# A transformer block with attention and experts: the first norms of batches 1 to 3 share their statistics, and norms, square sums, reciprocals and projections are issued in smaller pieces

## The reference, cut to what matters

```python
x = x + attention(layernorm(x))          # layernorm over the 128 features, eps 1e-5
def attention(z):
    k, q, v = z @ Wk, z @ Wq, z @ Wv     # 16 heads of 8
    k = head_norm(k) * kln_w + kln_b     # over the 8 features of each head
    q = head_norm(q) * qln_w + qln_b
    dot = einsum(q, k) / sqrt(8), causal mask, softmax over keys
    return einsum(softmax, v) @ Wo + bo
```

## Time and profile before

| | us |
|---|---|
| median of 3 timed runs | 2811.04 (2809.29 to 2815.23) |
| the profiled execution's own time | 2812.77 |
| its span | 2811.0 |
| TensorE busy | 2606.5 (93%) |
| VectorE busy | 1777.8 (63%) |
| ScalarE busy | 1602.0 (57%) |
| GpSimd busy | 819.7 (29%) |

### The profile page before, as it was taken

One profiled execution on the slowest core, in us unless ns is written; L12 is line 12 of the kernel. 1 busy time (PEld: TensorE's weight loads), 2 busy tenths in 40 slices (PEclk: granted clock), 3 DMA queues, 4 the chain that ended last, 5 costly groups with the idle time before them and its releaser, 6 DMA issues. The chain is left out here.

```text
span 2811.0 us, 54937 instructions
## 1 busy us (share of the span) xinstructions
PE 2606.5 (93%) x18814; PEld 1697.9 (60%) x18814; DVE 1777.8 (63%) x4103; ACT 1602.0 (57%) x2918; POOL 819.7 (29%) x1181
## 2 busy tenths in 40 slices
PE   5899998988599889999999999999999999995997
PEld 3555565554488745565555556555555555554886
DVE  7777777784566655555655556555556655556666
ACT  2666666776544455555555556565566555554443
POOL 4152423426154311111111111122122123322642
PEclk7999999999899989999999999999999999998998
DMA  6500000001434268888888888877888788885222
GB/s 110 87 12 16 16 16 9 16 13 35 124 121 149 74 153 199 196 195 194 202 194 196 195 195 191 187 181 180 188 189 194 181 201 200 202 202 197 72 87 86
DMA packets 193508, 383.24 MB, mean 136 GB/s; under 512 B 46305, under 2 KB 101738, under 8 KB 191882
## 3 DMA queue, kind: packets, MB, share of 16 engines
q1 hardware_dynamic: 184650, 362.55, 54.1%
q0 software_dynamic: 8640, 17.84, 1.8%
HBM read 38.10 MB, written 39.86 MB: 28 GB/s over the span
## 5 line engine op out<-in xcount | busy, mean ns | idle before, releaser
L3060 DVE STREAM_TRANSPOSE m_turned<-m_sig 128x1024 f32<-128x1024 f32 x512 | 613.6, 1227 | 434.0 <-ACT m_sig L2816 198.7
L2653 PE MATMUL m_v_ps<-m_sig,m_tok 128*64 128x512 f32 x2048 | 468.3, 599 | 0.0
L2666 PE MATMUL m_v_ps<-m_sigT,m_tok 128*64 128x256 f32 x4064 | 461.7, 380 | 3.7 <-DMA m_sigT<-m_turned 3.4
L2637 PE MATMUL m_f_ps<-m_swap,m_own 64*128 64x512 f32 x1536 | 426.1, 404 | 16.4 <-DMA m_swap<-m_own 8.2
L885 ACT ACTIVATE a_prob<-a_bank 128x512 f32<-128x512 f32 (+1 forms) x640 | 328.5, 568 | 175.5 <-PE a_bank L703 172.6
L2637 PE MATMUL m_f_ps<-m_own,m_swap 64*128 64x512 f32 x1536 | 426.3, 404 | 0.0
L2666 PEld LDWEIGHTS m_v_ps<-m_sigT,m_tok 128*64 128x64 f32 x4064 | 289.2, 137 | 202.1 <-issue 52.6
L2926 POOL TENSOR_TENSOR m_own<-m_uv,m_own 128x1024 fp32r<-128x1024 f32 x64 | 152.0, 2374 | 816.4 <-ACT m_own L2792 816.4
L2830 ACT ACTIVATE m_sig<-m_f_ps 128x1024 f32<-128x1024 f32 x256 | 248.3, 1022 | 246.0 <-issue 148.2
L2637 PEld LDWEIGHTS m_f_ps<-m_swap,m_own 64*128 64x128 f32 x1536 | 271.6, 186 | 99.9 <-ACT m_sig L2816 25.9
L2653 PEld LDWEIGHTS m_v_ps<-m_sig,m_tok 128*64 128x64 f32 x2048 | 135.8, 137 | 265.4 <-issue 265.0
(11 more groups left out here) (507 smaller groups left out, 4318.4 us busy)
## 6 DMA issues: line engine op xcount, KB each, us to landing
m_sigT<-m_turned SPq DMA_DIRECT2D x2042, 128.0 KB, 2.3
m_swap<-m_own SPq DMA_DIRECT2D x64, 256.0 KB, 3.3
f_t_rows<-f_sent_rows SPq DMA_DIRECT2D x142, 65.0 KB, 2.0
f_sent_rows<-a_proj SPq DMA_DIRECT2D x34, 260.0 KB, 8.8
k_apart<-a_kT SPq DMA_DIRECT2D x128, 64.0 KB, 2.0
m_swap<-m_own SPq DMA_DIRECT2D x64, 128.0 KB, 3.2
f_h<-back_rows SPq DMA_DIRECT2D x8, 512.0 KB, 5.0
rows<-back_rows SPq DMA_DIRECT2D x6, 512.0 KB, 4.2
```

The source lines that it names most:

```text
L2637: mm = pe.matmul(f_ps[s][:, cols], tile_of(u[rows, :], j + s * SIDE), v[rows, cols], start=start, stop=stop)
L2653: mm = pe.matmul(v2_ps[h * RANK:(h + 1) * RANK, :], tok[p][:, 0, j + s * SIDE, :], sig[j % 2][s][:, h * HALF:(h + 1) * HALF], start=(j == ...
L2666: mm = pe.matmul(v1_ps[h * RANK:(h + 1) * RANK, g * 2 * P:(g + 1) * 2 * P], tok[p][:, 1, jj, :], sigT[g][:, :, 2 * h:2 * h + 2, jj, :].rea ...
L3060: dve.transpose(turned[g][:, :, q, :, :], sig[j % 2][s][:, :].rearrange("p (t j a) -> p j t a", j=4, a=STACK)).then_inc(turn_ready, 1)
```

## The change

- The statistics of the 24 tiles of batches 1 to 3 are taken in the first group, two tiles at each of the slots 8, 10, ..., 30; moments, root and reciprocal for all 24 follow once, at slots 33, 35 and 37 of the same group. They live in the buffers of the later norms (`x_mean`, `x_dev`, `x_rstd`, `stats`), which nothing else uses at that time.
- The norm of a batch is issued in four pieces of two tiles at slots 1, 3, 5 and 7 of g = 1; the turns are at slots 10 and 12; the projections one at a time at slots 14, 16, 18, 21, 23, 26, 29 and 31. Before the first of them ScalarE waits for the stacked queries of the batch before.
- In g = 2 the square sums of the keys are at slot 5 and those of the queries at slot 6, each with its own scaling; the reciprocal of the keys stays at slot 9, that of the queries is at slot 14. The opening does the same in halves.

```diff
+        STATS_AT = tuple(range(8, 32, 2))
+        PROJECT_AT = (14, 16, 18, 21, 23, 26, 29, 31)
...
+                if first and i in STATS_AT:
+                    yield "token_stats", STATS_AT.index(i)
+                if first and i in (33, 35, 37):
+                    yield ("token_moments", "token_dev", "token_rstd")[(33, 35, 37).index(i)], 0
                 if prep and g == 1:
-                    if i in (1, 3, 5):
-                        yield ("token_stats", "token_dev", "token_norm")[i // 2], 0
-                    if i in (13, 15):
-                        yield "turn_z", i // 15
-                    if i in (21, 23, 26, 29):
-                        for n in range(2):
-                            yield "project", 2 * (21, 23, 26, 29).index(i) + n
-                if prep and g == 2 and i in (0, 2, 5, 7, 9, 10, 12, 20, 21):
-                    yield {0: ("square", 1), 2: ("square", 0), 5: ("square_sums", 0), 7: ("head_dev", 0), 9: ("head_rstd", 0),
-                           10: ("affine", 1), 12: ("stack_keys", 0), 20: ("affine", 0), 21: ("stack_queries", 0)}[i]
+                    if i in (1, 3, 5, 7):
+                        yield "token_norm", i // 2
+                    if i in (10, 12):
+                        yield "turn_z", i // 12
+                    if i in PROJECT_AT:
+                        yield "project", PROJECT_AT.index(i)
+                if prep and g == 2 and i in (0, 2, 5, 6, 7, 9, 10, 12, 14, 20, 21):
+                    yield {0: ("square", 1), 2: ("square", 0), 5: ("square_sums", 1), 6: ("square_sums", 0), 7: ("head_dev", 0), 9: ("head_rstd", 1),
+                           10: ("affine", 1), 12: ("stack_keys", 0), 14: ("head_rstd", 0), 20: ("affine", 0), 21: ("stack_queries", 0)}[i]
...
-            def projected(u, t):
+            def projected(u, nb, t):
                 src = u.next()
                 u.wait_full(act)
+                if nb and t == 0:
+                    act.wait_ge(queries_ready, GROUPS * nb)
...
-                pool.wait_ge(rstd_ready, nb + 1)
+                pool.wait_ge(rstd_ready, 2 * nb + 2 - a)
...
+            def token_stats(n):
+
+                if n == 0:
                     dve.wait_ge(x_in, 16 * (BATCH - 1))
+                for t in range(TILES + 2 * n, TILES + 2 * n + 2):
+                    ins = dve.bn_stats(k["stats"][:, t, :], k["x"][:, t * DIM:(t + 1) * DIM])
+                return ins
+
+            def token_moments(link):
+                row_moments(dve, link, k["stats"][:, TILES:, :], later_mean, later_dev, later_work, ALL - TILES).then_inc(token_var, 1)
+
+            def token_rstd(link):
+                dve.wait_ge(token_dev_ready, 1)
+                link(dve.reciprocal(later_rstd, later_dev))
+
+            def token_norm(nb, n):
+                for t in range(2 * n, 2 * n + 2):
+                    at = nb * TILES + t
+                    ins = dve.tensor_scalar(z[:, t, :], x_tile(nb, t), k["x_mean"][:, at:at + 1], k["x_rstd"][:, at:at + 1], ALU.subtract, ALU.mult)
+                if n == TILES // 2 - 1:
+                    ins.then_inc(z_ready, 1)
+
+            def square_sums(link, nb, a, heads=slice(0, HEADS)):
+                dve.wait_ge(squares_ready, 2 * nb + 2 - a)
+                link(dve.tensor_reduce(qk_var[:, a, :, heads], qk_sq[:, a, :, heads, :], AX.X, ALU.add))
+                var = qk_var[:, a, :, heads]
                 dve.tensor_scalar(var, var, 1.0 / HD, EPS, ALU.mult, ALU.add).then_inc(var_ready, 1)
 
+            def head_rstd(nb, a, heads=slice(0, HEADS)):
+                dve.wait_ge(dev_ready, nb + 1)
+                dve.reciprocal(qk_rstd[:, a, :, heads], qk_dev[:, a, :, heads]).then_inc(rstd_ready, 1)
```

More of the change, by code:

```diff
@@ L351, in sem @@
             return sems[-1]
-        stats, mean, spread, work, dev, rstd, z = (k[n] for n in ("a_stats", "a_mean", "a_spread", "a_work", "a_dev", "a_rstd", "a_z"))
+        z = k["a_z"]
         zT = sb("a_zT", [P, SEQ])
@@ L844, in _, with token_dev @@
         def _(act):
-            def token_dev(nb):
-                act.wait_ge(var_ready, 2 * nb)
-                act.activation(dev[:, :], spread[:, :], ACT.Sqrt).then_inc(dev_ready, 1)
+            def token_dev():
+                act.wait_ge(token_var, 1)
+                act.activation(later_dev, later_dev, ACT.Sqrt).then_inc(token_dev_ready, 1)
             def first_head_dev():
@@ L961, in _ @@
                 empty_z(u, tiles)
-            made = [projected(u, t) for t in range(TILES)]
+            made = [projected(u, 0, t) for t in range(TILES)]
             first_head_dev()
@@ L1128, in x_tile @@
                 return k["x"][:, ds((nb * TILES + t) * DIM, DIM)]
-            def token_stats(link, nb):
-                if not (isinstance(nb, int) and nb == 0):
+            def token_stats(n):
+                if n == 0:
                     dve.wait_ge(x_in, 16 * (BATCH - 1))
[L1133 to L1142, removed]
-                ins.then_inc(z_ready, 1)
-            def square_sums(link, nb, heads=slice(0, HEADS)):
-                dve.wait_ge(squares_ready, 2 * nb + 2)
-                for a in range(2):
-                    ins = dve.tensor_reduce(qk_var[:, a, :, heads], qk_sq[:, a, :, heads, :], AX.X, ALU.add)
-                link(ins)
-                var = qk_var[:, :, :, heads]
+                for t in range(TILES + 2 * n, TILES + 2 * n + 2):
+                    ins = dve.bn_stats(k["stats"][:, t, :], k["x"][:, t * DIM:(t + 1) * DIM])
@@ L1151, in square_sums @@
+            def square_sums(link, nb, a, heads=slice(0, HEADS)):
+                dve.wait_ge(squares_ready, 2 * nb + 2 - a)
+                link(dve.tensor_reduce(qk_var[:, a, :, heads], qk_sq[:, a, :, heads, :], AX.X, ALU.add))
+                var = qk_var[:, a, :, heads]
                 dve.tensor_scalar(var, var, 1.0 / HD, EPS, ALU.mult, ALU.add).then_inc(var_ready, 1)
-            def head_rstd(nb, heads=slice(0, HEADS)):
-                dve.wait_ge(dev_ready, 2 * nb + 1)
-                dve.reciprocal(qk_rstd[:, :, :, heads], qk_dev[:, :, :, heads]).then_inc(rstd_ready, 1)
+            def head_rstd(nb, a, heads=slice(0, HEADS)):
+                dve.wait_ge(dev_ready, nb + 1)
+                dve.reciprocal(qk_rstd[:, a, :, heads], qk_dev[:, a, :, heads]).then_inc(rstd_ready, 1)
@@ L1422, in group @@
                     elif what == "token_stats":
-                        token_stats(link, b + 1)
+                        ins = token_stats(n)
+                        if n == len(STATS_AT) - 1:
+                            link(ins)
+                    elif what == "token_moments":
+                        token_moments(link)
+                    elif what == "token_rstd":
+                        token_rstd(link)
                     elif what == "token_norm":
-                        token_norm(link, b + 1)
+                        token_norm(b + 1, n)
                     elif what == "square_sums":
-                        square_sums(link, b + 1)
+                        square_sums(link, b + 1, n)
                     elif what == "head_rstd":
-                        head_rstd(b + 1)
+                        head_rstd(b + 1, n)
                     elif what == "half_moments":
@@ L1466, in _ @@
             stack_first(link)
-            square_sums(link, 0, slice(GROUP, HEADS))
-            head_rstd(0, slice(GROUP, HEADS))
+            for a in (1, 0):
+                square_sums(link, 0, a, slice(GROUP, HEADS))
+            for a in (1, 0):
+                head_rstd(0, a, slice(GROUP, HEADS))
             u.n += 4
```

9 lines of the change are left out of this document (6 added, 3 removed).

## The result

The changed kernel takes 2792.18 us (median of 5 runs, 2791.66 to 2796.8) beside 2811.04 of the kernel before (2807.39 to 2815.53, 5 runs on the same chip). The ratio is 0.9941, 95% interval 0.9928 to 0.9954: 16.6 us less (12.9 to 20.2), where 9.5 was forecast.

What follows compares the result with a forecast made beforehand. TensorE is busy 93% of the span, so only its waits and low clock can be won. Token-norm groups -13.0, first group +3.5, rest 0: -9.5 us, from 2812.8 to 2803.3 (2801.5 for the median); range 2793 to 2811.

Steps and rivals of the forecast that it cites:

- the first token-norm stretch: Sign: the token-norm groups' first stretch, to the finished heads, takes 16 to 18 us with two projections in it.
- the one wait in the first group: Sign: TensorE has one wait of at most 2 us in the first group.
- that group's growth: Sign: the first group is 3 to 4 us longer; growth over 8 us would refute the forecast.
- Those of the square-sum groups: Signs: first TensorE wait booked to ScalarE, group length as before; a change over 1.5 us each would refute it.
- Token-norm groups: Batches 1 to 3: 19.9 us of waits and low clock, less 6.9 kept, gain 13.0 us.
- the 1.5 us that the norm's wait was to keep: Token-norm groups: TensorE's wait caused by the norm, now 1.39 to 1.54 us, left at 1.5 each despite splitting.
- The 0.3 for the turn: Token-norm groups: turn at slot 10 waits for the norm ending at slot 7; 0.3 us each, between 0 and 0.65.
- One norm held by GpSimd per group: Token-norm groups: one norm piece lengthened beside GpSimd's stacking, 0.48 us per group, between 0 and four such surpluses.
- the rival with four held pieces: Rival 2: GpSimd holds all norm pieces in the token-norm groups, 4.3 us more cost, 2806; chance 0.1.
- The rivals that put 12.1 us there: First group costs 12.1 us: rival 3, no change, 2810, chance 0.16; rival 4, VectorE absorbs nothing, 2827, chance 0.1.
- the step "0.7 - 0.87, three times: nothing": Square-sum groups: root on ScalarE 0.7 us later against first reciprocal halved, saving 0.87; no gain over three groups.
- Rival 1: Square-sum groups gain too, 1.35 for a sum plus 0.87 for the reciprocal per batch: 6.7 us more, 2795; chance 0.2.

Runs made afterwards that it cites:

- e6: Changed kernel with only the shared statistics: norm whole at slot 5, turns 13 and 15, projections in pairs, sums at 5, reciprocals at 9; 0.9952.
- e2: Changed kernel with the norm of a batch whole at slot 7 instead of four pieces; 2794.43 us, 0.9949.
- e4: Changed kernel with both square sums at slot 5, reciprocals still apart at slots 9 and 14; 2793.29 us, 0.9939.
- e8: Changed kernel with the heads' root at slot 13, keys' reciprocal, scaling and stacking from 14, queries' reciprocal at 16; 2794.68 us, 0.9944.
- e12: Changed kernel: statistics at 0, 4; moments, root, reciprocal at 16, 20, 22; sums together; keys' reciprocal at 11; buffer clearing after second group; 2790.41 us, 0.9930.
- e11: Kernel before with the heads' whole reciprocal at slot 11, behind the shift, instead of slot 9; 2802.33 us, 0.9974.
- e1: Kernel before with the halves alone: square sums at slots 5 and 6, reciprocals at 9 and 14, opening in halves too; 2805.18 us, 0.9983.
- e3: Changed kernel with turns at slots 13 and 15 and projections in pairs, as before the change; 2792.42 us, 0.9935.
- e5: Changed kernel with both reciprocals at slot 9, the keys' first, sums at 5 and 6; 2794.98 us, 0.9948.

## Why the prediction was right, and where it was short

1. **Direction and place: right.** The shared statistics carry the gain: e6 alone has 0.9952. The waits of some 3.3 us at the start of the token-norm groups are gone. Of the signs that the prediction named for itself, the first token-norm stretch (16.57 us for 16 to 18), the one wait in the first group (1.46 for at most 2) and that group's growth came true. Those of the square-sum groups did not: their first wait is still booked to VectorE, and two of the three changed by more than 1.5 us (2.68, 1.63, 1.12).
2. **Token-norm groups: mechanism right, size off, 17.9 for 13.0.** A group without any wait would be 33.24 + 1.3 for the turns + 5.07 for the projections = 39.6 us; these are 40.02, 40.48 and 40.45, so 0.4 to 0.9 is left each where I left 2.3, and 3 x 1.6 is the difference. The mis-sized term is the 1.5 us that the norm's wait was to keep. It is 0.65 to 1.2 of waits with the split norm and 1.6 with the whole one (e2). In these two traces the clock stays at 1.00 behind it; in the second group of e4, e8 and e12, with the same waits, it was low for 3.4 us, and the group took 41.5 us instead of 40.5. The 0.3 for the turn was not needed either: TensorE doesn't wait for a piece there. TensorE's turns and projections, moved ahead of slot 17, let VectorE catch up. The prediction said this and put no number on it; undone together with the split, it is 3.9 us in the traces (e6 against the changed kernel). That splitting wins little by itself was right. One norm held by GpSimd per group, 0.48 longer than the others, is there in the second and third group, at the first of the four pieces (VectorE of the changed kernel); the kernel before had one such norm in each group too (812 to 817 ns), inside its 2.61 us, so it was no added cost:

```profile
257.70 1.20 DVE L1159 TENSOR_SCALAR a_z<-x,x_mean,x_rstd 128x128 f32<-128x128 f32 x2
259.85 0.59 DVE L1159 TENSOR_SCALAR a_z<-x,x_mean,x_rstd 128x128 f32<-128x128 f32 x2
```

   So the rival with four held pieces, which the quoted rule of the Trainium skill (SBUF — State Buffer, "Who interferes with whom") would give if each piece met GpSimd, did not happen.
3. **First group: right, 3.87 for 3.5.** VectorE's idle time took up what fitted, one wait of 1.46 us stands at the moments and the root. The rivals that put 12.1 us there did not happen.
4. **Square-sum groups: the step "0.7 - 0.87, three times: nothing" failed; they won 5.4.** Its parts were right (the root later by 0.7, the half reciprocal 0.8 shorter), the sum was not: I subtracted them from each other as if both stood on one path. The 0.7 lie in the wait for ScalarE. The 0.8 come off a row of VectorE, reciprocal then held shift, that overran TensorE's lead, and the whole wait of 0.99 to 1.63 us behind it went. I had the held shift among my rows and used it as a caution against the norm pieces only. e6 and e11 show it: with the shift held for less or not at all, that wait goes although the reciprocals stay whole or together. Net of what grew elsewhere TensorE stands still 1.7 us less in the three groups. The step also put the low clock at nothing: it is 6.8 us less, some 2 us by the price above (an estimate), and the remaining 1.7 us of the 5.4 are not assigned to either. That the edit itself brings less low clock is not shown, as e1, the same code in these groups, has it for 13.7 us and the changed kernel for 17.1. Rival 1 had the right groups and came nearest in the number (2795), with the wrong reason: e4 shows that the sums' separation wins nothing.
5. **Projections one at a time: nothing alone**, within the error (e3, with the turns late too: 1.5 us in the trace and none in the timed runs), as forecast.

The sum of the forecast counted the low clock in one place only, the excess of the token-norm groups, and there it did go (20.5 us to none). The bounds took time at the low clock as half lost; here 3.4 us of it cost 1.0, not 1.7.

What stays open: 1.35 us of the opening, which the traces of kernels with and without its halves end between 65.2 and 66.8, and why the low clock lasts 0 to 10.2 us in a square-sum group after waits that are much alike. The busy time of TensorE also holds waits too short to be shown apart (it grew by 1.6 us in the first group at the same clock), so the split into wait and clock is rough.

## What to carry to other kernels

Sum up an engine's bursts over the lead of the ring, not one by one: two operations of 1.75 and 1.51 us a unit apart waited as one, and taking 0.8 us from either removed the whole wait in most groups. Count what grew elsewhere against it, and split the gain into waits and clock before comparing two traces: e11 looked better than e1 by 1.5 us and had no fewer waits. An operation far longer than its usual time (1.51 for 0.18 us) is to be read as a wait for another engine, and moving it ahead of what releases that engine cost no wait for that engine here (e11); started later still (e8), it was waited for 1.9 us. Before shortening the stage that waits, look at the queue of the next transfer: with the first group shortened, the next wait was for a DMA behind eighteen others.

## What the runs showed of the hardware

- A TENSOR_SCALAR of 16 columns on VectorE takes 0.18 us alone, and 1.51 or 0.70 us when GpSimd's TENSOR_TENSOR of 1.98 us has begun 0.5 or 1.3 us before it; it ends when that one does. A RECIPROCAL (0.88 us in e5, the second half) and the maxima (0.63 us at 161.50 in the kernel before) beside the same GpSimd operation are not held.
- After TensorE's waits of 3.3 and 1.5 us the token-norm stretches had a granted clock of 0.77 to 0.92; after waits of 0.2 to 1.0 us it is 1.00 in all three of the changed kernel. It is no rule: in e4 the second token-norm group has waits of the same length and a granted clock of 0.51 from 260.9 to 264.2. The square-sum stretches, with 1.2, 1.3 and 1.0 to 1.25 us in a row, still fall to 0.50 (the 1.2 GHz level), from 305.1 to 311.8 in the second; in e11 the first of them stays at 1.00 throughout after waits of 2.33, 0.78 and 0.67 us.
- ScalarE goes through another table and back in 2.8 us where it waits for nothing: in the changed kernel from the load at 102.13, with a root of 0.22 us between the two loads, to the next exponential at 104.96.
